# A fused decoder kernel: the feed-forward stage without the sum on GpSimd

## The reference, cut to what matters

```
vals   = FP4_LUT[codes]                          # 4-bit codes
w_gu   = vals_gu * scale_gu                      # a scale per group of 128 inputs, per output
gate_up = einsum('bsh,oh->bso', x, w_gu)         # x: 8 x 256 tokens, 512 features
gate, up = gate_up[..., :1408], gate_up[..., 1408:]
h = silu(gate) * up
y = einsum('bsi,hi->bsh', h, w_down)
return y / sqrt(mean(y*y) + eps)
```

## Time and profile before

| | us |
|---|---|
| median of 3 runs | 2489.37 |
| lowest and highest of the runs | 2486.86 to 2494.13 |
| the profiled execution, its own time | 2480.99 |
| its span in the trace | 2479.2 |
| the feed-forward stage in the trace, first matmul to the last `copy_y` | 2083.2 to 2415.9 |
| busy in the whole span: PE, DVE, ACT, POOL | 1917.2, 1767.4, 1202.2, 863.0 |

### The profile page before, as it was taken

One profiled execution on the slowest core, in us unless ns is written; L12 is line 12 of the kernel. 1 busy time (PEld: TensorE's weight loads), 2 busy tenths in 40 slices (PEclk: granted clock), 3 DMA queues, 4 the chain that ended last, 5 costly groups with the idle time before them and its releaser, 6 DMA issues. The chain is left out here.

```text
span 2479.2 us, 33578 instructions
## 1 busy us (share of the span) xinstructions
PE 1917.2 (77%) x12096; PEld 1241.4 (50%) x12204; DVE 1767.4 (71%) x2601; ACT 1202.2 (48%) x2131; POOL 863.0 (35%) x518
## 2 busy tenths in 40 slices
PE   2788774307299999998677999988984767799996
PEld 1447653304276677775464767664541324344444
DVE  4339995795877888887574465663545998999976
ACT  0013322554377888887522233233445865466654
POOL 1014444220235888886451222241001002343330
PEclk8988886658699999999898999998996987999998
DMA  4223645201246999999730000021335320000002
GB/s 153 68 102 109 225 165 191 87 0 19 93 164 209 250 260 259 263 245 288 206 147 1 1 1 1 1 119 52 102 102 203 138 76 1 0 1 1 1 1 68
DMA packets 118421, 271.00 MB, mean 109 GB/s; under 512 B 29105, under 2 KB 53169, under 8 KB 114546
## 3 DMA queue, kind: packets, MB, share of 16 engines
q1 hardware_dynamic: 100562, 226.15, 26.3%
q0 software_dynamic: 17696, 42.72, 8.5%
HBM read 191.76 MB, written 78.15 MB: 109 GB/s over the span
## 5 line engine op out<-in xcount | busy, mean ns | idle before, releaser
L1493 DVE SCALAR_TENSOR_TENSOR x_part<-x_group,x_scale,x_part 128x256 f32<-128x256 f32 (+1 forms) x660 | 263.8, 441 | 105.6 <-ACT x_part L1435 96.7
L1379 PE MATMUL x_group<-x_xt,x_gu 128*128 128x256 f16 (+1 forms) x2640 | 314.5, 261 | 26.5 <-ACT x_part L1435 14.3
L1435 ACT ACTIVATE x_part<-x_group,x_scale 128x256 f32<-128x256 f32 (+1 forms) x660 | 255.1, 445 | 56.5 <-PE x_group L1379 56.2
L1379 PEld LDWEIGHTS x_group<-x_xt,x_gu 128*128 128x128 fp8e4 x2640 | 232.8, 99 | 75.0 <-ACT x_part L1435 15.5
L1344 POOL TENSOR_TENSOR x_part<-x_part 128x512 f32<-128x512 f32 (+1 forms) x165 | 204.8, 1249 | 139.6 <-DVE x_part L1493 138.7
L2497 POOL TENSOR_TENSOR f_part<-f_part 128x1024 f32<-128x1024 f32 x44 | 120.4, 2737 | 187.0 <-DVE f_part L2524 187.0
L170 PE MATMUL mean_n<-residual,const_tables 128*128 128x256 f32 x320 | 78.8, 400 | 135.3 <-PEq L767 99.2
L1832 POOL TENSOR_TENSOR c_pt<-c_pt,const_tables 128x1024 f32<-128x1024 f32 x32 | 75.9, 2371 | 260.1 <-ACT c_pt L1806 260.1
L2395 PE MATMUL f_group<-f_x_hi,f_raw 128*128 128x512 f16 x352 | 138.4, 393 | 33.1 <-DVE f_part L2524 25.6
L2261 ACT ACTIVATE z_pt<-z_s 128x1024 f32<-128x1024 f32 x128 | 119.7, 1054 | 51.1 <-PE z_s L2232 50.0
L2524 DVE SCALAR_TENSOR_TENSOR f_part<-f_group,f_scale,f_part 128x512 f32<-128x512 f32 x176 | 123.9, 742 | 26.0 <-ACT f_part L2446 20.6
(11 more groups left out here) (337 smaller groups left out, 4874.9 us busy)
## 6 DMA issues: line engine op xcount, KB each, us to landing
x_d_hi<-down_hi SPq DMA_DIRECT2D x50, 768.0 KB
x_gu<-codes_gu SPq DMA_DIRECT2D x50, 384.0 KB, 4.9
x_d_lo<-down_lo SPq DMA_DIRECT2D x50, 384.0 KB
p_w<-d_s SPq DMA_DIRECT2D x17, 768.0 KB, 7.0
down_hi<-p_hi SPq DMA_DIRECT2D x17, 768.0 KB, 4.5
aux<-ct SPq DMA_DIRECT2D x2, 4096.0 KB, 13.4
cross_values<-y_v_out SPq DMA_DIRECT2D x16, 512.0 KB, 3.1
z_v_st<-cross_values SPq DMA_DIRECT2D x8, 1024.0 KB, 7.7
```

Of the source, the lines that this page charges most:

```text
L1379: mm = pe.matmul(group_ps[s % 2][:, q, columns(j)], codes[:, q, col:col + P], xt[u][:, k, q, columns(j)], start=k == 0, stop=k == 1)
L1435: act.activation(part[n % PARTS][:, q, o % 2, columns(j)], group_ps[s % 2][:, q, columns(j)], ACT.Copy, scale=scale[v][:, o, q:q + 1]).the ...
L1493: dve.scalar_tensor_tensor(x, group_ps[s % 2][:, 2 + q, columns(j)], scale[v][:, o, 2 + q:3 + q], x, ALU.mult, ALU.add).then_inc(ev_dve, 1)
```

## The change

ScalarE copies only bank 0 of each half. VectorE adds banks 1, 2 and 3 to that copy in turn, each waiting for the one before it through VectorE's own semaphore. GpSimd's add and the semaphore `summed` are gone, `part` is half as large, and `silu` waits for the third addition of the gate half. TensorE waits for `ev_act` ahead of bank 0 only, and for `ev_dve` ahead of the other three. GpSimd keeps `split_w` and issues its eleven instructions one after the other, with nothing between them.

```diff
@@ tensor: groups
-                        pe.wait_ge((ev_act, ev_dve)[c // 2], 2 * (H - 1) + c % 2 + 1)
+                        if c == 0:
+                            pe.wait_ge(ev_act, H)
+                        else:
+                            pe.wait_ge(ev_dve, 3 * (H - 1) + c)
@@ scalar: groups, silu
-                for c in range(2):
-                    act.wait_ge(group_done, C * (2 * N + k) + c + 1)
-                    act.activation(part[N % PARTS][:, c, k, :], group_ps[c][:, :], ACT.Copy,
-                                   scale=scale[:, N % G_F, k, c:c + 1]).then_inc(ev_act, 1)
+                act.wait_ge(group_done, C * (2 * N + k) + 1)
+                act.activation(part[N % PARTS][:, k, :], group_ps[0][:, :], ACT.Copy,
+                               scale=scale[:, N % G_F, k, 0:1]).then_inc(ev_act, 1)
-                act.wait_ge(summed, N + 1)
-                x = part[N % PARTS][:, 0, 0, :]
+                act.wait_ge(ev_dve, 6 * N + 3)
+                x = part[N % PARTS][:, 0, :]
@@ gpsimd
             split_w(0)
-            for N in range(LAST):
-                x = part[N % PARTS]
-                pool.wait_ge(ev_dve, 4 * (N + 1))
-                pool.tensor_tensor(x[:, 0, :, :], x[:, 0, :, :], x[:, 1, :, :], ALU.add).then_inc(summed, 1)
-                if N + 1 < G_F:
-                    split_w(N + 1)
+            for n in range(1, G_F):
+                split_w(n)
@@ vector: groups, product
-                for c in range(2, C):
-                    dve.wait_ge(group_done, C * (2 * N + k) + c + 1)
-                    dve.wait_ge(ev_act, 2 * (2 * N + k) + c - 1)
-                    x = part[N % PARTS][:, c - 2, k, :]
+                H = 2 * N + k
+                for c in range(1, C):
+                    dve.wait_ge(group_done, C * H + c + 1)
+                    if c == 1:
+                        dve.wait_ge(ev_act, H + 1)
+                    else:
+                        dve.wait_ge(ev_dve, 3 * H + c - 1)
+                    x = part[N % PARTS][:, k, :]
                     dve.scalar_tensor_tensor(x, group_ps[c][:, :], scale[:, N % G_F, k, c:c + 1], x, ALU.mult, ALU.add)\
                        .then_inc(ev_dve, 1)
                 dve.wait_ge(silu_done, N + 1)
+                dve.wait_ge(ev_dve, 6 * (N + 1))
-                dve.tensor_tensor(h[N % 2][:, :], x[:, 0, 0, :], x[:, 0, 1, :], ALU.mult).then_inc(h_done, 1)
+                dve.tensor_tensor(h[N % 2][:, :], x[:, 0, :], x[:, 1, :], ALU.mult).then_inc(h_done, 1)
```

More of the change, by code:

```diff
@@ L2365, in feed_forward @@
         x_hi, x_lo = two("x_hi", [P, C, TT], F16), two("x_lo", [P, C, TT], F16)
-        part = [sb(f"part{i}", [P, 2, 2, TT]) for i in range(PARTS)]
+        part = [sb(f"part{i}", [P, 2, TT]) for i in range(PARTS)]
         h = two("h", [P, TT])
@@ L2373, in feed_forward @@
         (ident_ready, turned, scale_ready, w_ready, w_high, w_split, x_high, x_ready, group_done, ev_act, ev_dve,
-         summed, silu_done, h_done, h_high, h_ready, h_used, y_copied, step_sem) = (
+         silu_done, h_done, h_high, h_ready, h_used, y_copied, step_sem) = (
             sem(n) for n in ("ident_ready", "turned", "scale_ready", "w_ready", "w_high", "w_split", "x_high",
-                             "x_ready", "group_done", "ev_act", "ev_dve", "summed", "silu_done", "h_done", "h_high",
+                             "x_ready", "group_done", "ev_act", "ev_dve", "silu_done", "h_done", "h_high",
                              "h_ready", "h_used", "y_copied", "step"))
```

## The result

The changed kernel took 2460.21 us (median of 4 runs, 2453.78 to 2466.93) against 2491.02 for the kernel before on the same chip: a ratio of 0.9878, with a 95% interval of 0.9847 to 0.9909. A second comparison of the same kernel, with more runs, gave 0.9893 (0.9871 to 0.9916). The forecast was 2463 us.

A forecast was written before the change was run, and what follows sets the result against it. VectorE set the pace (6.64 us a unit, TensorE needing 6.23). Gains of 1 (units 0, 1), 12.9 (2 to 8), 12.1 (9 to 43) and 0.5 (tail) make 26.5: 2489.4 - 26.5 = 2463 us, range 2451 to 2478.

The forecast's parts named there:

- GpSimd's add holds `product`: VectorE, later tiles: `product`, 0.68 us alone, lasts until GpSimd's add ends; removing the add returns 2.18 us a unit.
- The link: VectorE's chained additions: each waiting for the one before costs 0.78 us, bounds 0.66 and 0.83.
- Units 2 to 9: First tile, paced by VectorE: 7.86 us a unit, 57.2 us in all instead of 70.1, gain 12.9.
- Units 9 to 43: Later tiles, TensorE becomes the bound: 6.23 us a unit plus 6.8 unhidden, 218.6 us in all, gain 12.1.
- The banks: PSUM banks 1 to 3, freed in turn: bank 3 ready 0.25 us before TensorE wants it, holding up to a 0.84 link.
- The tail: After the last unit: `product(42)` no longer held, mostly taken by TensorE's last `down` matmuls; gain 0.5 us.
- Units 0 and 1: Start of the first tile, paced by TensorE at its lower clock: gain 1 us, bounds 0 and 1.7.
- Rival A: First tile: GpSimd's `split_w` falls on `low` or the shifts, costing up to 12.6 us; gain 14 to 20; chance 0.12.
- B: Later tiles: VectorE stays the bound, 6.32 us a unit at a 0.95 link; gain 15, 2474 us; chance 0.08.
- C: VectorE's chain of additions makes the kernel slower from links of about 1.1 us; 2502 us at 1.15; chance 0.03.
- D: Later tiles: `product` stays long, not GpSimd's doing; unit 7.82 us, 40 us lost, 2530 us; chance 0.02.
- E: Whole kernel: nothing measurable, gain under 7.5 us, from a link near 1.0 or two rivals together; chance 0.05.

The follow-up runs named there:

- the idle add: Changed kernel with GpSimd's old add back in the later tiles (units 11 to 43), on a tile nobody uses or waits for: 2523.77 us (one execution).

## Why the prediction was right, step by step

The kernel after has these marks at the first addition of units 2, 9 and 43 (the counterpart of the earlier trace rows):

```profile
2099.07 4.82 DVE L2526 SCALAR_TENSOR_TENSOR f_part<-f_group,f_scale,f_part 128x512 f32<-128x512 f32 x6
...
2158.43 4.82 DVE L2526 SCALAR_TENSOR_TENSOR f_part<-f_group,f_scale,f_part 128x512 f32<-128x512 f32 x6
...
2377.22 2.45 DVE L2526 SCALAR_TENSOR_TENSOR f_part<-f_group,f_scale,f_part 128x512 f32<-128x512 f32 x3
```

- **GpSimd's add holds `product`**: right in cause and size. 2.18 us a unit was forecast; the median fell from 2861 to 683 ns, and the idle add put it back. L2335 and L2338 went to 0.41 and 0.48 us as forecast. That the additions are not held was read from few cases, since before the change GpSimd's add starts only after the fourth addition; the kernel after shows it, with `split_w` beside additions of 753 ns at the most.
- **The link**: the term that was mis-sized. Taken at 0.78 us, with an upper bound of 0.83; it is 0.85. The row that I took it from the earlier trace rows has one wait ahead of the second instruction, the new additions have two, and the run with one wait gives 0.785. An addition also takes 0.750 us in the median rather than 0.741. The gap between linked additions is thus 0.10 us, just at the mark that the prediction named as a sign of being wrong: it had the mechanism right and this price too low. The rule of the Trainium skill weighed against that row (page "VectorE: DVE Perf Modes", section "The DRAIN you can't avoid"), that a semaphore after each of a chain of instructions costs nothing extra, does not hold for this shape: the unlinked additions follow every 0.66 us, the linked ones every 0.785 or 0.85.
- **Units 2 to 9**, VectorE's unit 7.86 us: it is 8.16, four links at 0.07 more. From 2099.07 to 2158.43 that is 59.4 us instead of 57.2: gain 10.7 where 12.9 was forecast.
- **Units 9 to 43**, TensorE as the bound at 6.23 us: right, and shown from both sides by the runs with less TensorE and with the unlinked addition. The mark moves from 2158.43 to 2377.22, 218.8 us against 218.6 forecast; the 6.8 us for `split_x` and `copy_y` measured 7.0. VectorE's gap before the up additions is 0.20 us, not 0.6: links again, hidden here. The banks held, but not by the 0.25 us that the prediction gave bank 3: by its own sum they hold up to a link of 0.84, the link is 0.85, and once a unit, in the up half, the weight load for bank 3 waits 0.32 us, just short of delaying its matmul.
- **The tail**: 0.2 us (2391.61 - 2377.22 = 14.39 against 14.55), not 0.5. **Units 0 and 1**, seen from each run's own first matmul: 2099.07 - 2084.53 = 14.54 against 2098.70 - 2083.19 = 15.51, gain 1.0 as forecast.
- **The sum**: 23.8 us in the stage against 26.5. The ratio of the medians allows for either. That the median came within 3 us of 2463 is in part luck: the medians differ by 30.8 us where the stage gained 23.8.
- **Rival A** (`split_w` collides) didn't happen here, by 0.5 us: 2111.48 against the end of the additions at 2112.05; it started 2.95 us after the first addition, and 3.0 was forecast. It happened in the run with the sum on VectorE, where the additions are shorter, at about 1 us a unit. **B** was half right in its cause, a dearer link, and the banks did lose their spare time, but VectorE's unit came to 5.93 us and stayed below TensorE's 6.23. **C** would have needed a link of 1.1. **D** is refuted by the idle add: moving work onto VectorE was right here because the work on GpSimd cost VectorE more. **E** is out with a gain of 23.8 against its 7.5.

## What to carry to other kernels

An instruction with two durations, one of them the length of a GpSimd instruction that runs beside it, may be held by that instruction: put the same instruction back on an idle tile to find out, and price the work on GpSimd by what it takes from VectorE, here 2.18 us for a sum that VectorE makes itself in 1.2. What moves off GpSimd needn't become a chain: two copies, two unlinked additions and one sum took less of the stage than one copy and three linked additions (300.0 against 307.1 us), and setting the rest of GpSimd's work beside instructions that read PSUM took another 7.4. When the price of a dependent instruction is taken from a row, count the waits ahead of it there and in the new place. A small error in such a price adds up: the 0.25 us that the sum of the banks had to spare was used up by four links that were 0.07 us dearer each.

## What the hardware showed unexpectedly

A second semaphore wait, already due, ahead of a VectorE addition that waits for the addition before it cost 0.06 us (a link of 0.85 against 0.785 us). Ahead of unlinked additions two waits cost nothing that shows (0.66 us from one to the next). And a single bank for each partial product makes a wait on the last bank dear: 0.70 us for the turn from VectorE's last read to TensorE's refilled bank, at the granted clock of 1.00, once a unit, ahead of the up half. The gate half has `low` and `product` ahead of it, which fill that time.
